# Sums of the first heads in two PSUM banks, merges 6 and 7 beside the LSTM steps, first tile's gates in two banks behind filler

## What is computed

```python
# hyperbolic transformer block, on tangent vectors of the ball (logmap0, expmap0)
xm   = expmap0(layer_norm(logmap0(x)) * (1 + sc_msa) + sh_msa)
q, k, v = heads(plin(xm, w_q)), heads(plin(xm, w_k)), heads(plin(xm, w_v))    # 16 heads of 16
attn = softmax(qt @ kt.T / sqrt(16)); out_h = expmap0(attn @ vt)
x1   = mobius_add(x, expmap0(g_msa * logmap0(plin(from_heads(out_h), w_o))))
ff   = plin(plin(modulated_norm(x1), w_f1), w_f2)                             # 256 -> 1024 -> 256
y    = x + mobius_add(x1, expmap0(g_mlp * logmap0(ff)))
# LSTM over the 512 rows, all 4 sequences at once, hidden size 256, h0 = cond
a = y_t @ Wx + b + h @ Wh;  i, f, o, g = gates(a);  c = f*c + i*g;  h = o*tanh(c)
out = y + h
```

## Time and profile before

| | us |
|---|---|
| median of 3 runs | 1542.81 (1541.64 to 1543.82) |
| the profiled execution | 1528.88 |
| its span, first to last instruction | 1527.1 |
| busy in the span: TensorE, weight loads | 1399.7 (92%), 1176.6 (77%) |
| busy: DVE, ScalarE, POOL | 1071.5 (70%), 869.6 (57%), 444.3 (29%) |
| mean granted TensorE clock | 0.966 of full |

### The profile page before, as it was taken

How to read it: one execution, slowest core, us unless ns; L and a number is a source line. 1 busy time by engine, 2 the same in 40 slices (tenths; PEclk the granted TensorE clock), 3 DMA queues, 4 the chain that set the end, 5 groups by cost and what they waited for, 6 DMA issues and landing times.

```text
span 1527.1 us, 65010 instructions
## 1 busy us (share of the span) xinstructions
PE 1399.7 (92%) x25442; PEld 1176.6 (77%) x25442; DVE 1071.5 (70%) x6339; ACT 869.6 (57%) x3236; POOL 444.3 (29%) x1198
## 2 busy tenths in 40 slices
PE   3895667699999999999999999999999999999998
PEld 2783334478788888888888888888888888788887
DVE  6895133467778788878887888787767676766665
ACT  2695566345466666666666666664544445454433
POOL 2331121232323434342424242525232232320000
PEclk9996888799999999999999999999999999999999
DMA  8000000000000000000000000000000000000000
GB/s 271 6 1 1 2 2 2 5 3 3 10 3 9 3 10 3 10 3 10 3 10 3 10 3 9 3 10 3 9 3 10 3 10 3 6 3 6 3 6 6
DMA packets 16715, 18.47 MB, mean 12 GB/s; under 512 B 6036, under 2 KB 15384, under 8 KB 16408
## 3 DMA queue, kind: packets, MB, share of 16 engines
q1 hardware_dynamic: 13016, 10.51, 2.3%
q10 hardware_dynamic: 3392, 3.81, 0.9%
HBM read 12.21 MB, written 2.10 MB: 9 GB/s over the span
## 4 chain that ended last, share of the span: by engine, by line
PE 65%; DVE 21%; issue 7%; ACT 5%; POOL 1%; DMA 1%; DVEq 0%; ACTq 0%; POOLq 0%
PE psum L824 27%; PE psum L863 18%; PE psum L799 3%; PE psum L764 3%; DVE cnew L1597 2%; ACT ot L1102 2%; PE psum L653 2%; DVE hl L1606 2%; PE psum L693 2%; PE psum L779 2%; DVE hl L1604 2%; PE psum L814 2%; PE psum L771 2%; ACT w L989 2%; DVE gO L1592 2%
## 5 line engine op out<-in xcount | busy, mean ns | idle before, releaser
L824 PEld LDWEIGHTS psum<-hl,wh 128*128 128x128 f16 x16384 | 469.8, 96 | 84.9 <-DVE hl L1606 77.0
L824 PE MATMUL psum<-hl,wh 128*128 128x8 f16 x16384 | 515.4, 172 | 14.8 <-DVE hl L1606 5.8
L863 PE MATMUL psum<-zeros,ident 128*128 128x256 f16 (+1 forms) x3389 | 417.3, 263 | 7.1 <-DVE gF L1590 1.1
L863 PEld LDWEIGHTS psum<-zeros,ident 128*128 128x128 f16 x3389 | 309.3, 98 | 78.6 <-DVE gF L1590 18.3
L1096 ACT ACTIVATE tA<-gA 128x16 f32<-128x16 f32 x512 | 110.7, 216 | 445.4 <-DVE gA L1588 445.4
L1588 DVE TENSOR_REDUCE gA<-psum 128x16 f32<-128x32 f32 x512 | 97.0, 190 | 136.7 <-PE psum L824 130.1
L1604 DVE TENSOR_TENSOR hl<-ot 128x8 f16<-128x8 f32 x512 | 90.0, 176 | 93.3 <-ACT ot L1102 92.9
L1102 ACT ACTIVATE ot<-cnew 128x8 f32<-128x8 f32 x512 | 109.7, 214 | 77.3 <-DVE cnew L1597 22.7
L1597 DVE TENSOR_TENSOR_SCAN cnew<-cmul,cadd 128x24 f32<-128x24 f32 x512 | 107.2, 209 | 29.0 <-DVE cadd L1594 1.7
L1606 DVE TENSOR_TENSOR_SCAN hl<-ot,hl 128x24 f16<-128x24 f32 x512 | 106.6, 208 | 17.8
L261 POOL TENSOR_TENSOR sc<-sc,cst 128x1 f32<-128x1 f32 (+1 forms) x146 | 106.3, 728 | 27.0 <-POOL sc L266 9.7
(11 more groups left out here) (311 smaller groups left out, 2280.2 us busy)
## 6 DMA issues: line engine op xcount, KB each, us to landing
arena<-in_x_dram SPq DMA_DIRECT2D x4, 512.0 KB, 9.1
wf<-in_L_cond_w_f_dram SPq DMA_DIRECT2D x2, 1024.0 KB, 19.5
xr<-in_x_dram SPq DMA_DIRECT2D x64, 32.0 KB, 1.8
out_dram<-place SPq DMA_DIRECT2D x64, 32.0 KB, 1.6
qv<-in_L_cond_w_ada_dram ACTq DMA_DIRECT2D x1, 1536.0 KB
oT<-in_L_cond_Wh_dram ACTq DMA_DIRECT2D x1, 1024.0 KB, 11.9
wx<-in_L_cond_Wx_dram SPq DMA_DIRECT2D x1, 1024.0 KB, 17.0
...
```

The costliest lines, as they stand in the source:

```text
L824: last = mm(cols, wh16[:, half, kc, (g0 + c) * P:(g0 + c + 1) * P], hl[:, :, kc, :, 2].rearrange("p e b -> p b e"), start=False, stop=c == ...
L863: mm(pF[:, D:D + n], ident16[:], zeros[:, 0:n], start=False, stop=False, skip_group_check=True)
```

## The change

- FIRST is -150, so heads 0 to 63 lie three slots earlier; heads 64 to 127 stay.
- The sums of tile k go to bank 2 or 7 by turns (`SUM_BANKS`); a tile waits for DVE's reading of the tile two back. The halves of a group are issued two slots later each, and ahead of the transposes back, which move from four to seven slots behind the last head; ScalarE's copy moves from three slots to six and behind the slot's exponentials.
- Merges 0 to 5 start nine slots after the last head. Merges 6 and 7 move to slots 18 to 31 and 50 to 63, with their arithmetic on POOL.
- Row tile 0's gates take two banks by turns, `pM` and `pP`, and each waits for the copy of the one two before; the second waits besides for ScalarE's reading of tile 1's transposes from `pP`.
- Row tile 1's first feed-forward products move from slots -7 to 1 to slots -1 to 3, the first of them behind the last gate copy, and its second ones start at slot 4 instead of 2.
- Filler products are added: six before the loop, one in each of the first eight slots, and 32, 8 and 4 in slots -13, -11 and -10, each lot behind a wait. Raised filler ends with step 1 instead of step 3.

```diff
@@ -70,19 +70,22 @@
-FIRST = -147
+FIRST = -150
 PAUSE = 65
...
 BATCHED = 2 * B * H
+MERGED_AHEAD = 6
 BEFORE_STEPS = -82
...
 WF1_AT = (26, 27, 28, 29, 30, 32, 33, 34)
+WF1_NEAR_START = (32, 33, 33, 34, 34, 35, 35, 36)
 WF2_AT = (35, 36, 37, 42, 42, 43, 43, 44)
+WF2_NEAR_START = (37, 38, 39, 42, 42, 43, 43, 44)
 GATES_AT = (57, 58, 59, 60, 61, 62, 63, 63)
@@ -96,9 +99,12 @@
-    return head_slot(H * k + H - 1) + 6
-
-
+    if k < MERGED_AHEAD:
+        return head_slot(H * k + H - 1) + 9
+    return RING * (k - MERGED_AHEAD) + 18 if k < 2 * B else head_slot(H * k + H - 1) + 6
+WARM_UP = {-13: ("n_xa2", 1, 32), -11: ("n_ab2", 2, 8), -10: ("n_x3", 1, 4)}
 HEAD_AT = {head_slot(n): n for n in range(HEADS)}
@@ -107,6 +113,14 @@
     [(RING * n + RING + 4, 3, ("out", n)) for n in range(NT)])]
+def wf1_at(n):
+    return WF1_NEAR_START if n == 1 else WF1_AT
+def wf2_at(n):
+    return WF2_NEAR_START if n == 1 else WF2_AT
@@ -233,6 +247,8 @@
+        SUM_BANKS = (pV, pA)
         def half_words(i):
@@ -323,6 +339,12 @@
         WLOADS = 6
+        def gate_rows(n, gi):
+            if n == 0:
+                return (pM, pP)[gi % 2][:, gi // 2 % 2 * P:(gi // 2 % 2 + 1) * P]
+            return pM[:, gi % 4 * P:(gi % 4 + 1) * P]
@@ -425,14 +447,14 @@
                 F = lambda name: num(name, 2 * H)[:, k % 2 * H:(k % 2 + 1) * H]
-                if k < 2 * B:
+                if k < MERGED_AHEAD:
                     if r == 3:
...
                 if r == 5:
-                    hold(pool, "t_rd", 2 * k - 2 * B + 2)
+                    hold(pool, "t_rd", k + 1 if k < 2 * B else 2 * k - 2 * B + 2)
                     ch.link(g.tensor_tensor(num("rd2", H), F("rd"), F("rd"), ALU.mult))
@@ -634,8 +656,11 @@
+            pe.wait_ge(s["h0_s"], 1)
+            pe.wait_ge(s["dinit"], 7)
+            for i in range(6):
+                mm(pO[:, 0:D], ident16[:], zeros[:], start=True, stop=True, skip_group_check=True)
             pe.wait_ge(s["ld_w"], 16 * WLOADS)
-            pe.wait_ge(s["h0_s"], 1)
             pe.wait_ge(s["p_kc"], NT)
@@ -685,12 +710,12 @@
                     pe.wait_ge(s["t_e"], first + 4)
-                    if first % H == 0 and k >= 1:
-                        pe.wait_ge(s["t_u"], k)
+                    if first % H == 0 and k >= 2:
+                        pe.wait_ge(s["t_u"], k - 1)
                 for kc in (2 * half, 2 * half + 1):
...
                         h = m % H
-                        last = mm(pV[32 * (h % 4):32 * (h % 4) + HD + 1, h // 4 * P:(h // 4 + 1) * P], vs[:, k % B, kc, h, :],
+                        last = mm(SUM_BANKS[k % 2][32 * (h % 4):32 * (h % 4) + HD + 1, h // 4 * P:(h // 4 + 1) * P], vs[:, k % B, kc, h, :],
                                   w32[:, m % 8, kc * P:(kc + 1) * P], start=kc == 0, stop=kc == NB - 1, skip_group_check=True)
@@ -699,18 +724,18 @@
                 for i in range(4):
-                    last = tr(pV[:, i * P:(i + 1) * P], oc[:, i * P:(i + 1) * P], ident[:])
+                    last = tr(SUM_BANKS[k % 2][:, i * P:(i + 1) * P], oc[:, i * P:(i + 1) * P], ident[:])
                 last.then_inc(s["t_T"], 1)
...
-                m = HEAD_AT.get(t - 4, HEADS)
+                for half in range(2):
+                    m = HEAD_AT.get(t - 6 - 2 * half, HEADS)
+                    if m < BATCHED and m % 4 == 0:
+                        four_weighted(m, half)
+                m = HEAD_AT.get(t - 7, HEADS)
                 if m < BATCHED and m % H == H - 1:
                     turned_back(m // H)
-                for half in range(2):
-                    m = HEAD_AT.get(t - 4 - 2 * half, HEADS)
-                    if m < BATCHED and m % 4 == 0:
-                        four_weighted(m, half)
                 m = HEAD_AT.get(t, HEADS)
@@ -755,17 +780,21 @@
                     last.then_inc(s["n_uT"], 1)
-                if r in WF1_AT:
-                    c = WF1_AT.index(r)
+                for c in range(KF):
+                    if r != wf1_at(n)[c]:
+                        continue
                     pe.wait_ge(s["n_uc"], n + 1)
-                    if c > 0:
-                        pe.wait_ge(s["n_fc"], KF * n + c)
+                    first = wf1_at(n).index(r)
+                    if first > 0:
+                        pe.wait_ge(s["n_fc"], KF * n + first)
+                    if n == 1 and c == 0:
+                        pe.wait_ge(s["n_xc"], GC)
                     for kc in range(KD):
...
                 for kc in range(KF):
-                    if r == WF2_AT[kc]:
+                    if r == wf2_at(n)[kc]:
                         if kc == 0:
@@ -792,11 +821,15 @@
                             wait_pM("gates", n)
-                        elif GATES_AT[gi - 1] < r:
+                        elif n == 0 and gi >= 2:
+                            pe.wait_ge(s["n_xc"], gi - 1)
+                        elif n > 0 and GATES_AT[gi - 1] < r:
                             pe.wait_ge(s["n_xc"], GC * n + gi)
+                        if n == 0 and gi == 1:
+                            pe.wait_ge(s["n_uc"], 2)
                         c = CHUNK[gi]
                         for kc in range(KD):
-                            last = mm(pM[:, gi % 4 * P:(gi % 4 + 1) * P], wx[:, kc, c * P:(c + 1) * P], XT[:, kc, :],
+                            last = mm(gate_rows(n, gi), wx[:, kc, c * P:(c + 1) * P], XT[:, kc, :],
                                       start=kc == 0, stop=kc == KD - 1, skip_group_check=True)
@@ -807,6 +840,7 @@
                     pe.wait_ge(s["w_lo"], GC)
+                    pe.wait_ge(s["t_u"], 2 * B)
                 at_ = i % (2 * RING)
@@ -849,12 +883,12 @@
                     if r < ROW_TILE and 0 <= (t + PAUSE - r) // RING < NT:
-                        cols += 1024 * ((r in (1, 2)) + (38 <= r < 42) + (r in WF1_AT) + WF2_AT.count(r) + GATES_AT.count(r)) + 256 * (r in (25, 56))
+                        cols += 1024 * ((r in (1, 2)) + (38 <= r < 42) + wf1_at((t + PAUSE - r) // RING).count(r) + wf2_at((t + PAUSE - r) // RING).count(r) + GATES_AT.count(r)) + 256 * (r in (25, 56))
                 return cols
...
-                wanted = RAISE if t < 4 or t % 64 == 23 and t < HEADS_END else BESIDE
+                wanted = RAISE if t < 2 or t % 64 == 23 and t < HEADS_END else BESIDE
                 lacking = wanted - beside(t)
@@ -867,6 +901,14 @@
                 pieces(t, attention, merged, post, out_rows)
+                if t in WARM_UP:
+                    done, value, products = WARM_UP[t]
+                    pe.wait_ge(s[done], value)
+                    pe.wait_ge(s["t_e"], BATCHED)
+                    for i in range(products):
+                        mm(pF[:, 0:D], ident16[:], zeros[:], start=True, stop=True, skip_group_check=True)
+                if t < FIRST + 8:
+                    mm(pP[:, 0:D], ident16[:], zeros[:], start=True, stop=True, skip_group_check=True)
                 if 0 <= t < T - 1:
@@ -973,12 +1015,6 @@
-                m = HEAD_AT.get(t - 3, HEADS)
-                if m < BATCHED and m % H == H - 1:
-                    act.wait_ge(s["t_AV"], m + 1)
-                    if m // H >= 1:
-                        act.wait_ge(s["t_T"], m // H)
-                    A(oc, pV, ACT.Copy).then_inc(s["t_c"], 1)
                 scale = 1.0 / (math.sqrt(HD) * QK_UP * QK_UP)
@@ -987,6 +1023,13 @@
                         A(w32[:, n % 8, :], (bank[0], bank[1], pF, pO)[n % 4], ACT.Exp, scale=scale).then_inc(s["t_e"], 1)
+                m = HEAD_AT.get(t - 6, HEADS)
+                if m < BATCHED and m % H == H - 1:
+                    act.wait_ge(s["t_AV"], m + 1)
+                    if m // H >= 1:
+                        act.wait_ge(s["t_T"], m // H)
+                    A(oc, SUM_BANKS[m // H % 2], ACT.Copy).then_inc(s["t_c"], 1)
+                m = HEAD_AT.get(t, HEADS)
                 n = HEAD_AT.get(t - 1, 0)
@@ -1057,9 +1100,10 @@
                     A(uT[:, 0, :, :].rearrange("p c t -> p (c t)"), pP[:, 0:D], ACT.Copy).then_inc(s["n_uc"], 1)
-                if r in WF1_AT:
-                    c = WF1_AT.index(r)
-                    act.wait_ge(s["n_f"], KF * n + c + 1)
+                for c in range(KF):
+                    if r != wf1_at(n)[c]:
+                        continue
+                    act.wait_ge(s["n_f"], KF * n + c + 1 + wf1_at(n)[c + 1:].count(r))
                     if n >= 1 and c == 0:
@@ -1085,8 +1129,8 @@
                     if r == GATES_AT[gi]:
-                        act.wait_ge(s["n_g"], GC * n + gi + 1 + GATES_AT[gi + 1:].count(r))
-                        A(xw[:, gi, :, n % 2 * RING:(n % 2 + 1) * RING], pM[:, gi % 4 * P:(gi % 4 + 1) * P].rearrange("p (b t) -> p b t", b=B),
+                        act.wait_ge(s["n_g"], GC * n + gi + 1 + (GATES_AT[gi + 1:].count(r) if n > 0 else 0))
+                        A(xw[:, gi, :, n % 2 * RING:(n % 2 + 1) * RING], gate_rows(n, gi).rearrange("p (b t) -> p b t", b=B),
```

(10 more changed lines are left out.)

## The result

The changed kernel takes 1490.7 us (median of 4 runs, 1490.3 to 1492.0) beside 1542.2 for the kernel before in the same comparison (4 runs, 1528.8 to 1543.8). The ratio is 0.969, 95% interval 0.963 to 0.974.

A forecast was written before the change was run, and what follows sets the result against it. Before the steps, waits between engines leave none full and lower TensorE's clock; then come 512 steps of 2.39 us. Savings 24.2 + 3 + 2 + 6.6 + 0.3 = 36.1 us, taken off the 1542.8 median: 1506.7 us, range 1497 to 1523.

The forecast's parts named there:

- the last one of the sum: Whole kernel: saving of 36.1 us applied unchanged to the runs' median of 1542.8, giving 1506.7 us.
- Rival (d): Start of the steps: clock falls, 1.2 us more a step, slower overall, 1607 if lasting to step 87; chance 0.03.
- Part 1: Attention slots before the first output product: scores issued ahead of sums, in two banks, save 24.2 us.
- The clock as granted after two groups: Heads 0 to 79: two groups at half clock, 18 at full, 43.7 us instead of 71.8.
- Part 2: First output product to row tile 0's last dot product: saves 3 us up to the first feed-forward product, then 2.
- Part 3: Tail, from row tile 0's last dot product to put_round: no wait for merge 7's power, alternating gates; saves 6.6 us.
- Part 4: The 512 LSTM steps: less raised filler and lighter step 0 against merges 6 and 7 moved in; net -0.3 us.
- (a): First stage, before the first output product: clock stays at half, saving only 19 us, 1524; chance 0.12.
- (b): Row chain before the steps keeps its present time except merge 7's 3.24 us wait: saving 27.7, 1515; chance 0.20.
- (c): Row chain before the steps shrinks too, middle stretches and tail at their best: saving 43.5, 1499; chance 0.15.
- (e): Attention slots: scores still wait for sums through a misread ring; only some 3 us saved, 1540; chance 0.04.

The follow-up runs named there:

- part 1 alone: Kernel before with only the earlier FIRST, later two-bank sums and later merges; merges 6 and 7 ahead of the steps, one gate bank, no added filler: 1504.4 us.

## Why the prediction was wrong

**The step that failed is the last one of the sum**: "The runs' median is 13.9 us above it at 1542.8, for a reason that the trace doesn't show; I take the saving as the same there." The sum before it comes out, 1492.8 for the like of the profiled execution and 1490.85 measured, though in part by luck: parts 1 to 3 gave 4.5 us more than forecast, and part 4 gave 2.6 less. The 13.9 us were no constant of the measurement. They were thirteen steps at half clock behind a late step 8, in most executions of the kernel before and by chance not in the one profiled. Rival (d) had the mechanism: the clock falls in the early steps, and every step then takes longer, by 1.2 us (measured 0.95). I gave it 0.03 as a thing that the change might cause, and argued against it from a clock of 1.00 in the one execution, when the same page's time stood 13.9 us, 13 steps of 1 us, below the median. The change, which takes raised filler away from steps 2 and 3, didn't bring the fall; in the changed kernel it is rare (1 of 10).

Term by term:

- **Part 1**, right in mechanism, 24.2 forecast and 26.8 found at the first output product. A group takes 2.14 to 2.22 us where 2.09 was worked out, and none runs at half clock, so that 20 of them come to about the 43.7 us of the sum; the losses that I booked against it (1.6 for heads 60 to 63, 1.8 for the merge, 0.5 for turns) were together some 2.5 us too high. "The clock as granted after two groups" is what the run without fillers shows (full from 140.8); with them it is up at the first exponential, for no gain at the output product.
- **Part 2**, 3 and 2 forecast, 3.6 and 2.7 found. The first is almost all part 1's doing, as the run of part 1 alone shows. Of the second, merge 6's absence gives 1.6 (29.6 us with the merges back, 28.0 without), as the prediction named it.
- **Part 3**, 6.6 forecast, 7.1 found. The shares were 3.2 for merge 7 and 3.4 for the gates; measured they are about 4.7 and 2.7. The 32 fillers count in it: without any filler the tail has a granted clock of 0.64 and is 1.3 us longer.
- **Part 4**, +0.3 forecast, -2.3 found. Steps 0 to 3 went as said (10.5 forecast, where the terms add up to 10.7; 10.39 found), and steps 20 and 52 grew by 0.10 and 0.32 where 0.6 a merge was booked. What was missing is a thing that no step of the prediction looks at: the merges' instructions left VectorE's queue ahead of the steps, 31 fewer records stand there, and all later ones are counted differently against the blocks of 128. That cost 2.9 us of the 3.7 that moving the merges cost the steps; the merges themselves are 0.7, step 0 gives 0.35 back, and some 0.4 is not found. So moving the merges gained 5.3 us ahead of the steps and lost 3.7 in them; the 1.6 left are less than the ten executions of the changed kernel are apart.
- The Trainium skill's rule of "SBUF — State Buffer", "Who interferes with whom", by which POOL's powers would hold VectorE's scans, doesn't show here either: 25 scans of the changed kernel start while a 16-column power runs on POOL, and they take 0.21 us each, like the 999 others. The steps of the two moved powers, 23 and 55, did not grow, and no step of these merges grew by more than 0.32 us, where a power takes 2.94.
- **The other rivals**: (a) fell, the clock came up at 136.3; (b) fell, the tail gave more than merge 7's wait; (c), 43.5, was more than the 38.0 found, and its 1499 lies nearer to the measured time than the forecast only because of the 13.9 us; (e) fell.
